# A graph network on one core: the gathers of the third layer read one table instead of two

## The reference

```python
x = x + rgcn(h)       # sum over edges of norm * h[src] @ W[etype], W from 8 bases
x = x + gcn2(h)       # two normalized graph convolutions, ReLU between
x = x + messages(h)   # the layer of the change, below
x = x + sage2(h)      # two mean aggregations, tanh between

# messages(h), F = 32 channels
hs = xs @ w_in2f_s / sqrt(128); hv = einsum(xv, w_in2f_v) / sqrt(128)
s, v = hs[dst], hv[dst]                  # idx_j is dst here: rows of u, 128 wide
Wij = (ssp(f_ij @ W1 + b1) @ W2 + b2) * rcut
edge = products of s, v, Yr_ij and Wij   # 32 x 16 values, from 8 distinct blocks of 32
agg = segment_sum(edge, src, n)          # idx_i is src
x += output of four small products of agg
```

## Time and profile before

| | |
|---|---|
| median of three runs | 1455.31 us (1454.26 to 1457.48) |
| profiled execution | 1456.16 us, its span 1454.3 us, mean granted clock 0.984 |
| TensorE busy | 1364.6 us, 94% of the span |
| GpSimd busy | 892.1 us, 61% |
| VectorE busy | 861.3 us, 59% |
| ScalarE busy | 494.5 us, 34% |
| gathers of h_rows (line 874) | 313, 303.0 us busy |
| scatters to slots (line 900) | 313, 315.1 us busy |
| gathers of u (line 930) | 243, of these 12 from `u_soon` |

### The profile page before, as it was taken

One profiled execution on the slowest core, in us unless ns is written; L12 is line 12 of the kernel. 1 busy time (PEld: TensorE's weight loads), 2 busy tenths in 40 slices (PEclk: granted clock), 3 DMA queues, 4 the chain that ended last, 5 costly groups with the idle time before them and its releaser, 6 DMA issues. The chain is left out here.

```text
span 1454.3 us, 24122 instructions
## 1 busy us (share of the span) xinstructions
PE 1364.6 (94%) x6924; PEld 937.1 (64%) x6925; DVE 861.3 (59%) x2485; ACT 494.5 (34%) x1279; POOL 892.1 (61%) x927
## 2 busy tenths in 40 slices
PE   4888799999999999999999989998999979999998
PEld 2778788888885444444694866665666656686565
DVE  8778755555554667776433429988888854411111
ACT  7000000000005888882521235654555546311100
POOL 5777777777777777777777767777777720000000
PEclk9999999999999999999999989999999989999999
DMA  4678789888885652233211122222222330000000
GB/s 164 193 228 232 237 288 312 259 239 257 269 263 159 171 163 83 76 84 110 57 26 26 37 60 59 71 65 64 74 67 65 87 77 1 30 0 30 8 29 35
DMA packets 104166, 172.96 MB, mean 119 GB/s; under 512 B 20155, under 2 KB 54128, under 8 KB 104080
## 3 DMA queue, kind: packets, MB, share of 16 engines
q0 software_dynamic: 42832, 103.15, 24.2%
q10 hardware_dynamic: 27790, 39.30, 8.8%
q1 hardware_dynamic: 33458, 29.39, 6.5%
HBM read 153.74 MB, written 18.02 MB: 118 GB/s over the span
## 5 line engine op out<-in xcount | busy, mean ns | idle before, releaser
L874 POOL DMA_INDIRECT gath<-h_rows,idx x313 | 303.0, 968 | 95.0 <-issue 66.8
L1008 PEld LDWEIGHTS ps<-spread,gath 128*128 128x128 f32 x2504 | 306.9, 197 | 73.8 <-issue 43.4
L1008 PE MATMUL ps<-spread,gath 128*128 128x96 f32 x2504 | 313.0, 281 | 24.6 <-DMA gath<-h_rows,idx 17.7
L1030 PE MATMUL ps<-base_t,z 128*128 128x512 f32 (+1 forms) x640 | 308.4, 603 | 0.0
L930 POOL DMA_INDIRECT u<-u_rows,at x219 | 218.6, 998 | 66.8 <-issue 63.4
L1550 DVE TENSOR_TENSOR z<-z,ps 128x384 f32 x313 | 172.7, 552 | 100.1 <-PE ps L1008 88.5
L900 POOL DMA_INDIRECT slots<-att,idx_s x160 | 161.6, 1010 | 49.5 <-issue 47.6
L1221 PE MATMUL ps<-msg,hot 128*128 128x256 f32 x648 | 162.4, 394 | 20.6 <-DVE msg L1922 19.5
L900 POOL DMA_INDIRECT slots<-z,idx_s x153 | 153.5, 1003 | 43.9 <-issue 41.2
L1221 PEld LDWEIGHTS ps<-msg,hot 128*128 128x128 f32 x648 | 119.2, 192 | 81.0 <-DVE msg L1922 59.8
L1030 PEld LDWEIGHTS ps<-base_t,z 128*128 128x128 f32 (+1 forms) x640 | 107.3, 188 | 75.1 <-issue 74.9
(11 more groups left out here) (297 smaller groups left out, 1837.8 us busy)
## 6 DMA issues: line engine op xcount, KB each, us to landing
base_t<-in_bases_dram ACTq DMA_DIRECT2D x116, 256.0 KB
slots<-att SPq DMA_DIRECT2D x21, 256.0 KB, 5.2
at<-slots SPq DMA_DIRECT2D x21, 256.0 KB, 2.7
gath<-h_rows,idx POOLq DMA_INDIRECT x313, 4.2
u<-u_rows,at POOLq DMA_INDIRECT x219, 2.5
att<-in_attr_dram SPq DMA_DIRECT2D x40, 64.0 KB
slots<-att,idx_s POOLq DMA_INDIRECT x160
z<-in_attr_dram SPq DMA_DIRECT2D x39, 64.0 KB
```

The costliest lines, as they stand in the source:

```text
L874: nc.gpsimd.indirect_dma_start(out=gath[:, c % RING, :], out_offset=None, in_=h_rows, in_offset=bass.IndirectOffsetOnAxis(ap=idx[:, par, c ...
L1008: last = mm(bank[:, k * SPREAD:(k + 1) * SPREAD], gath[:, h_slot, k * P:(k + 1) * P], s_of.rearrange("p b d -> p (b d)"), start=True, stop ...
L1030: return mm(ps[BANKS[n]][0:rows(n), :], z[:, k, b, n * P:n * P + rows(n)], base_t[:, k, :], start=(t == JOINS[n]), stop=(t == JOINS[n] + T ...
```

## The change

The table `u_soon`, its five stores, its semaphore and the two conditions are taken out. All 243 gathers read `u_rows`, and the first waits, as the others did, for the ten stores of `u_rows`. The matrix of conditions is two columns narrower. Everything that isn't shown is the same.

```diff
@@ -63,7 +63,6 @@
 ETS = 8
 SLICES = CHUNKS // QUAD // ETS
 NEAR_CHUNKS, SELF = 94, 8
-SOON, SOON_BLOCKS, SOON_CHUNKS = 4, 5, 215
 DONE_BY = [106, 148, 180, 207, 231]
 JOINS = [0, 20, 26, 52, 52, 84, 84, 84, 84, 84]
 BANKS = [4, 5, 6, 3, 4, 0, 1, 2, 3, 4]
@@ -101,7 +100,6 @@
     x1_rows = nc.dram_tensor("x1_rows", (HALF * P, FEAT), f32).ap()
     slots = nc.dram_tensor("slots", (SLOTS, ROW), f32).ap()
     u_rows = nc.dram_tensor("u_rows", (NODES, P), f32).ap()
-    u_soon = nc.dram_tensor("u_soon", (SOON_BLOCKS * P, P), f32).ap()
 
     ctx = ExitStack()
     with ctx:
@@ -174,13 +172,12 @@
         pid = sb(part, "pid", [P, 1], f32)
         pid_i = sb(part, "pid_i", [P, 2], i32)
         inside = sb(part, "inside", [P, 1], f32)
-        near_n = sb(part, "near_n", [P, BLOCKS + 3 + HALF], f32)
-        near_b = sb(part, "near_b", [1, BLOCKS + 4 + HALF], f32)
+        near_n = sb(part, "near_n", [P, BLOCKS + 1 + HALF], f32)
+        near_b = sb(part, "near_b", [1, BLOCKS + 2 + HALF], f32)
         part.close()
         tmp_a, tmp_b, tmp_i = gath[:, 7, 0:CHUNKS], gath[:, 6, 0:CHUNKS], gath[:, 5, 0:CHUNKS].bitcast(i32)
         win_f, col_id = gath[0:1, 4, 0:CHUNKS], gath[:, 3, 0:P]
         near_hot = gath[:, 0, :].bitcast(bf16)[:, 0:BLOCKS * NEAR_CHUNKS].rearrange("p (s t) -> p s t", s=BLOCKS)
-        soon_hot = gath[:, 1, :].bitcast(bf16)[:, 0:SOON_CHUNKS]
         next_i, rising = gath[:, 2, 0:CHUNKS].bitcast(i32), gath[:, 1, 0:CHUNKS]
         coef_scope.close()
         part = ExitStack()
@@ -287,7 +284,6 @@
 
         ld_tab, ld_wc, ld_bias, st_h, st_zero, ld_w12, st_u, ld_mp, ld_mq, ld_x1 = semaphores(
             "ld_tab ld_wc ld_bias st_h st_zero ld_w12 st_u ld_mp ld_mq ld_x1")
-        st_soon = sem("st_soon")
         ld_x = semaphores("ld_xp0 ld_xp1 ld_xp2 ld_xp3 ld_xp4")
         ld_et, ld_norm, row_ok, sel_ok, et_ok, et_pe, wc_ok, wc_up, wc_low = semaphores(
             "ld_et ld_norm row_ok sel_ok et_ok et_pe wc_ok wc_up wc_low")
@@ -765,8 +761,6 @@
                         .then_inc(u_ev, 1)
                     act.wait_ge(u_ev, m + 1)
                     act.dma_start(u_rows[m * P:m * P + r, :], u_out[0:r, m, :]).then_inc(st_u, 16)
-                    if m < SOON_BLOCKS:
-                        act.dma_start(u_soon[m * P:m * P + r, :], u_out[0:r, m, :]).then_inc(st_soon, 16)
             radial(*at_step(-4))
             act.wait_ge(ld_mp, 16 * 13)
             radial(*at_step(-3))
@@ -914,11 +908,7 @@
                     if not valid(st):
                         return
                     there, used = in_reg(pool, lap16(st, s8)), in_reg(pool, st - RING + 1)
-                    soon = bool(skip) and isinstance(st, int) and st < SOON
-                    if soon:
-                        pool.wait_ge(st_soon, 16 * SOON_BLOCKS)
-                    else:
-                        pool.wait_ge(st_u, 16 * BLOCKS)
+                    pool.wait_ge(st_u, 16 * BLOCKS)
                     pool.wait_ge(ld_at[s8 // QUAD], there)
                     after(pool, m_ok, used)
                     if s8 % QUAD == 1 and not (isinstance(st, int) and st < QUAD):
@@ -928,7 +918,7 @@
                     at_i = at[:, s8 // QUAD, s8 % QUAD, :, :].bitcast(i32)
                     for c in range(skip, QUAD):
                         nc.gpsimd.indirect_dma_start(
-                            out=u_ring(st)[:, s8, c + 1 - skip, :], out_offset=None, in_=u_soon if soon else u_rows,
+                            out=u_ring(st)[:, s8, c + 1 - skip, :], out_offset=None, in_=u_rows,
                             in_offset=bass.IndirectOffsetOnAxis(ap=at_i[:, c, DSTC:DSTC + 1], axis=0))\
                             .then_inc(u_in[s8], 16)
 
@@ -987,7 +977,7 @@
                 j, half = i // 2, i % 2
                 if i == BLOCKS:
                     pe.wait_ge(cnt_in, 3)
-                    mm(ps[6][0:1, 1:BLOCKS + 4 + HALF], ones[:, 0:1], near_n[:, :], start=True, stop=True).then_inc(cnt_pe, 1)
+                    mm(ps[6][0:1, 1:BLOCKS + 2 + HALF], ones[:, 0:1], near_n[:, :], start=True, stop=True).then_inc(cnt_pe, 1)
                 pe.wait_ge(et_hot, i + 1)
                 if i >= 6:
                     pe.wait_ge(coef_ok, j - 2)
@@ -1454,7 +1444,7 @@
             dve.wait_ge(dve_o, n_v.n)
             v.tensor_scalar(acol[:, :], tmp_a, -1.0, float(AWIN), ALU.max, ALU.min).then_inc(cnt_in, 1)
             dve.wait_ge(cnt_pe, 1)
-            v.tensor_scalar(near_b[0:1, BLOCKS + 3 + HALF:BLOCKS + 4 + HALF], ps[6][0:1, 0:1], EDGES - 0.5, None, ALU.is_ge)
+            v.tensor_scalar(near_b[0:1, BLOCKS + 1 + HALF:BLOCKS + 2 + HALF], ps[6][0:1, 0:1], EDGES - 0.5, None, ALU.is_ge)
 
             dve.wait_ge(ld_et, 16)
             v.tensor_copy(et_b[:, :], et_i[:, :]).then_inc(et_ok, 1)
@@ -1489,8 +1479,6 @@
                     for n in range(HALF):
                         v.tensor_scalar(near_n[:, BLOCKS + 1 + n:BLOCKS + 2 + n], dst_i[:, DONE_BY[n]:DONE_BY[n] + 1],
                                         (n + 1) * P - 0.5, float(SELF), ALU.is_ge, ALU.mult)
-                    v.tensor_scalar(near_n[:, BLOCKS + 1 + HALF:BLOCKS + 2 + HALF], dst_i[:, SOON_CHUNKS - 1:SOON_CHUNKS],
-                                    SOON_BLOCKS * P - 0.5, float(SELF), ALU.is_lt, ALU.mult)
                 if i == 2:
                     split_weights()
                 if i >= 3:
@@ -1502,23 +1490,18 @@
             v.tensor_tensor(near_hot, tmp_i[:, 0:NEAR_CHUNKS].unsqueeze(1).broadcast_to([P, BLOCKS, NEAR_CHUNKS]),
                             iota_w[:, 0:BLOCKS].unsqueeze(2).broadcast_to([P, BLOCKS, NEAR_CHUNKS]), ALU.is_equal)\
                 .then_inc(dve_o, n_v.up())
-            v.tensor_scalar(soon_hot, tmp_i[:, 0:SOON_CHUNKS], 0.0, None, ALU.is_equal).then_inc(dve_o, n_v.up())
             v.tensor_scalar(near_n[:, BLOCKS:BLOCKS + 1], dst_i[:, NEAR_CHUNKS - 1:NEAR_CHUNKS], P - 0.5, float(SELF),
                             ALU.is_lt, ALU.mult)
             dve.wait_ge(dve_o, n_v.n)
-            v.tensor_reduce(near_n[:, 0:BLOCKS], near_hot, mybir.AxisListType.X, ALU.add)
-            v.tensor_reduce(near_n[:, BLOCKS + 2 + HALF:BLOCKS + 3 + HALF], soon_hot, mybir.AxisListType.X, ALU.add)\
-                .then_inc(dve_o, n_v.up())
+            v.tensor_reduce(near_n[:, 0:BLOCKS], near_hot, mybir.AxisListType.X, ALU.add).then_inc(dve_o, n_v.up())
             dve.wait_ge(dve_o, n_v.n)
-            v.tensor_scalar(near_n[:, BLOCKS + 2 + HALF:BLOCKS + 3 + HALF], near_n[:, BLOCKS + 2 + HALF:BLOCKS + 3 + HALF],
-                            -(QUAD - 1.0) * SOON, None, ALU.add)
             v.tensor_scalar(near_n[:, BLOCKS - 1:BLOCKS], near_n[:, BLOCKS - 1:BLOCKS], 1.0, None, ALU.add)\
                 .then_inc(cnt_in, 1)
             for i in range(BLOCKS, 2 * SLICES + 2):
                 coefficients(i)
                 if i == BLOCKS:
                     dve.wait_ge(cnt_pe, 2)
-                    v.tensor_scalar(near_b[0:1, 0:BLOCKS + 3 + HALF], ps[6][0:1, 1:BLOCKS + 4 + HALF], SELF * P - 0.5, None, ALU.is_ge)\
+                    v.tensor_scalar(near_b[0:1, 0:BLOCKS + 1 + HALF], ps[6][0:1, 1:BLOCKS + 2 + HALF], SELF * P - 0.5, None, ALU.is_ge)\
                         .then_inc(dve_o, n_v.up())
                     dve.wait_ge(dve_o, n_v.n)
                     v.tensor_reduce(fit_f[:, :], near_b[:, :], mybir.AxisListType.X, ALU.min).then_inc(dve_o, n_v.up())
```

## The result

The kernel after takes 1462.72 us (median of 7 runs, 1456.80 to 1464.72), the kernel before 1454.97 in the runs beside it (7 runs, 1454.26 to 1457.48). The ratio is 1.0044, 95% interval 1.0030 to 1.0058: slower by 6.4 us, 4.4 to 8.4. The two medians are 7.8 us apart, within that interval. The profiled spans say the same, 1460.8 against 1454.3.

What follows compares the result with a forecast made beforehand. POOL's gather queue was taken to bound the message stage, VectorE waiting for it from step 18. Terms +9.1 - 4.3 + 0 - 0.6 = +4.2 us gave 1460.4 from the profiled execution, forecast 1459.5 after the median; range 1456.8 to 1464.3.

Steps and rivals of the forecast that it cites:

- rival A: Message steps: the gathers' delay is passed on less the avoided stalls, 1459.5 us, own range 1458.3 to 1461.2; chance 0.54.
- B: Message steps: all of the delay stays, long gathers recurring or the strict port rule holding; +8.5, 1463.8 us; chance 0.20.
- The start of the gathers (+9.1): Start of message steps: first gather waits for the tenth store, at 865.5 instead of 856.4; between +8.7 and +9.8 us.
- The lead is eaten first: Message steps: step 0 stays at 873.50, POOL's 12.0 us lead falls to 2.9; VectorE first waits at step 3 to 5.
- The pay-back (-4.3): Gathers from 882.3 to 936.6: stalls vanish once VectorE has gaps, 39 gathers at the later pace; bounds 0 and -6.3 us.
- the stall of 446.36: Nearest row for the mechanism: a VectorE memset of 2.69 us at 446.25 holds a GpSimd scatter, which takes 3.59 us.
- The early stalls stay.: Until 882, POOL loses about 1.2 us near 871.80 and 2.0 at 877.79; VectorE's work there doesn't move, so both stay.
- rival C: Early message steps: the stalls before 882 go too; no change, not slower, 1456.3 to 1457.5, say 1457.3 us; chance 0.22.
- ScalarE without stores (0): Second-table stores: five lie in ScalarE's waits, so the tenth store stays at 863.88; 0, at most -0.1 us.
- The condition (-0.6): Near 31 us: VectorE loses a compare, a sum and two small operations at the head of a chain; bounds -0.7 and 0.
- The collision and the clock (0): Weight loads near 1160.71 and VectorE's 4.03 us wait at 1168.69 move along at no cost; no clock change reckoned with.
- D: Edge stage: faster, as shifted gathers remove small stalls among its 313; would have to bring over 7 us; chance 0.02.

Runs made afterwards that it cites:

- the wait alone: Kernel before, with the first twelve gathers also waiting for all ten stores of u; second table, its stores and conditions stay: 1462.44 us, ratio 1.0049.
- late weights: Fourth layer's weight loads held until the last message step's gathers have landed: on the kernel before 1455.56 us, ratio 1.0003; on the kernel after 1459.92, ratio 1.0034.
- the groups: Profiles averaged: before, condition out, weights late, two extra VectorE works (start 857.1, queue 316.0) against after, wait alone, after with late weights (867.3, 312.2).
- gaps kernels: VectorE waits added at two places between message steps: on the kernel before 1451.53 us, ratio 0.9973; on the kernel after 1458.17, ratio 1.0023.
- wait and pause: Kernel before with first gathers waiting for all ten stores, plus three GpSimd memsets (about 4.5 us) ahead of the first gather: 1461.70 us, ratio 1.0047.

## Why the prediction was right, and where its size was off

The direction, the place and the mechanism held. Of size, +4.2 us were forecast and +6.4 measured against the runs beside it, inside the range; the median, 1462.72, is 3.2 above the 1459.5 forecast. It is also above the range that rival A had for itself (to 1461.2) and nearer to B's 1463.8, and +6.4 lies midway between A's +4.2 and B's +8.5. So the time alone doesn't choose between them; the shorter queue does. Point by point:

- **The start of the gathers (+9.1).** Right, and slightly too small. Forecast with the early gain: 864.9; measured 866.23. The tenth store was issued 1.2 us later than forecast with that gain (864.47), the way from its issue to the gather took 1.76 us instead of 1.62. The added wait alone reproduces the loss.
- **The lead is eaten first.** Right: step 0 of VectorE stood (+0.59), and the first wait for a gather came at step 4, forecast 3 to 5. The step number is partly luck, since it depends on how fast TensorE runs the first steps: the granted clock from 873 to 893 was 0.92 in this profile, steps 0 to 4 took 15.3 us and the first wait came at step 4; with the wait alone it was 0.66, 18.2 us and step 8, in the kernel after with late weights 0.75, 18.5 us and step 10. In step 3 VectorE starts without a wait, but only 2.66 us after its third gather's start, about the landing time.
- **The pay-back (-4.3).** Right in size and, up to one row, in its cause. In the pair of profiles POOL is 9.5 us late at step 6 and 5.1 at step 19, the range of the estimate; the whole queue is 4.94 shorter, 3.9 in the mean of the groups. What was wrong is the row taken as nearest for the mechanism: a memset of VectorE doesn't hold a gather (0.94 us beside one of 4.33); instructions with two SBUF inputs do. So the prediction's "the trace agrees on the stall of 446.36" doesn't stand either: what was laid beside a gather in the form of that row, a memset, didn't hold it. What held that scatter stays open. In all twelve profiles the scatter that starts beside this memset takes 3.44 to 3.64 us, and no experiment laid a memset beside a scatter. The row read as "beside the end of the last instruction of that run" is wrong too: the gather of 906.51 ends 0.24 us before that end, and 0.83 after the second sum. That gaps let the gathers through is shown by the gaps kernels: they remove the long gathers and make both kernels faster.
- **"The early stalls stay."** The one of 2.99 us did (3.00 at 878.38); near 871.80 stands a smaller one (1.49 at 872.59 for 1.69). In the kernel with wait and pause, whose queue starts 5.4 us later still, the long one goes too (no gather over 1.07 before 885). So what rival C lived on can happen, from a later start than this change gives. The reason given against it ("that run doesn't move") holds only while VectorE doesn't wait for POOL in that run.
- **ScalarE without stores (0).** Right within what the runs can tell: the five stores are gone, and the tenth still follows the pace of the blocks.
- **The condition (-0.6).** Not settled. Alone it measured -1.0 +- 1.6. In the profile after, the first edge product starts 0.3 earlier (45.10 for 45.40) and the last scatter 3.0 earlier (847.80 for 850.80), but the tenth store, which now bounds, is 0.6 later. Over the profiles of kernels whose code is the same up to the third layer, that store is issued between 862.58 and 867.86, so 0.6 can't be seen in it. The same holds for the sign that the prediction took as decisive, an edge stage that ends other than 0.6 us earlier. VectorE's last addition of the stage starts 1.1 us earlier after (443.24 for 444.36), which taken as written would make the prediction wrong; but in kernels with the same code for this stage it starts anywhere from 444.14 to 449.27. One pair of profiles can't decide it. A gain for GpSimd's scatters no longer counts: the change has moved the bound off them.
- **The collision and the clock (0).** This was the step with the least support. In the pair of profiles 1.9 us come between the last gather and step 80. Step 77's start moved with the gathers, as forecast (1174.20 for 1168.69), but then TensorE's clock was lower for longer in the kernel after. It falls in both behind this wait, between its two levels of 1.2 and 2.4 GHz: over 15 us, from 2.3 us ahead of the end of the wait, it is 0.77 on average after (1175 to 1190) and 0.89 before (1169.5 to 1184.5), with 0.50 against 0.66 in the first 5 us behind the wait and 0.89 against 1.00 in the next 5. The waits were nearly the same, 3.59 and 3.49 us. Timelines of PE, after and before:

```profile
1177.36 3.78 PE L1211 MATMUL ps<-msg,hot 128*128 128x256 f32 x8 [3.59 <-DVE msg L1905]
...
1181.79 1.82 PE L1187 MATMUL ps<-w_blk,hid 128*128 128x512 f32 x2
```

```profile
1171.84 3.09 PE L1221 MATMUL ps<-msg,hot 128*128 128x256 f32 x8 [3.49 <-DVE msg L1922]
...
1175.58 1.23 PE L1197 MATMUL ps<-w_blk,hid 128*128 128x512 f32 x2
```

 The longer fall doesn't belong to the change: the kernel with the wait alone has 5.88 us between last gather and step 80, as before, a clock of 0.89 in the same 15 us, and loses as much. So of the 2.2 us that the forecast lacks, the profiles give +1.35 for the start (1.2 for the store, 0.14 for the way to the gather), -0.6 for a larger pay-back, +1.9 in the last steps, where the clock stayed down longer, and -0.3 for the tail. In the means of the groups it is the start (10.2 instead of 8.5) and a pay-back of 3.9 for 4.3 alone. How much of it any one run would show is open; the interval of the measurement is itself 2 us wide to either side.

**The rivals.** B (all of the delay, +8.5) falls: the queue is shorter in every late kernel, and its +8.5 lies just outside the interval, which ends at 8.4; the time alone would be thin ground. The strict port rule that stood behind it does hold for one long instruction, and fails as a count of stalls. C and D fall with the interval's lower end at +4.4.

**What stays open.** Why one gather that starts in a stretch of two-input instructions is held to its end and another isn't. The constant 0.82 us between the end of the stretch and that of the gather suggests that it waits near its start, as that is all but some 0.13 of the usual 0.95. In the kernel with gaps the gather of 906.68 took 0.94 in the midst of a step of VectorE with two-input instructions, while in a run of 6.4 us the gather of 906.51, the last of four in it, waits for the end of the stretch. A run of one step lets gathers through and a double run holds its last; the runs don't say whether it is the number of gathers in it or their place.

## What to carry to other kernels

A lead that an engine has built up is worth less than its length when the engine that it feeds is full, since there the two hamper each other; price a delay of the queue's start as the delay less the stalls that it avoids, and look for them as single long instructions in a group whose mean is above the later one. Look for the gapless runs of the busy engine before counting its load: two waits that cost it tenths gave this kernel 0.27%, though each is added work for an engine at 92%. And a second copy of a table is paid by the wait that it avoids, not by the stores that it costs: here the stores lay in ScalarE's waits, and giving them up gave nothing that shows.

## What the runs showed of the hardware

- A VectorE memset of 4.33 us left the gathers of GpSimd at 0.94 us; two additions with both inputs in SBUF, 4.48 us together, held one for 4.36. The end of a held gather follows that of the last two-input instruction by 0.81 to 0.83 us, in 37 of 37.
- Long gathers come in a few sharp sizes, the same in different kernels (1.92 to 1.94 in eight, 2.32 in seven, 2.59 or 2.60 in five, 2.90 to 3.00 in two). With a gap between all steps of VectorE none over 1.45 us was left (two kernels).
- Behind a wait of about 3.5 us TensorE's granted clock fell in each kernel looked at, but by differing amounts: over the 15 us around the wait's end it was 0.89 before (3.49 us of waiting) and 0.89 with the wait alone (3.47), and 0.77 after (3.59). In the kernel with late weights a wait of 2.87 us in the last step, with little work behind it, was followed by ten microseconds at 0.50, where the kernel before had 0.68, and its tail was 2 us longer. A stall removed ahead of a stage can thus come back as slower clock in it.
